# Attention over sorted edges: a fixed schedule of steps in place of a schedule of windows

## The reference

```python
q = (feats @ Wq.T + bq).reshape(bs, NHEAD, HDIM).transpose(1, 0, 2)
k = (feats @ Wk.T + bk).reshape(bs, NHEAD, HDIM).transpose(1, 0, 2)
v = (feats @ Wv.T + bv).reshape(bs, NHEAD, HDIM).transpose(1, 0, 2)
r, c = (edge_index[:, 0], edge_index[:, 1])
qe = q[:, c, :]
ke = k[:, r, :]
ve = v[:, r, :]
sim = jnp.einsum('hed,hed->eh', qe, ke) * scale
m = jax.ops.segment_max(sim, c, num_segments=bs)
p = jnp.exp(sim - m[c])
s = jax.ops.segment_sum(p, c, num_segments=bs)
attn = p / s[c]
out_e = attn.T[..., None] * ve
out_e = out_e.transpose(1, 0, 2).reshape(-1, NHEAD * HDIM)
agg = jax.ops.segment_sum(out_e, c, num_segments=bs)
return agg @ Wo.T + bo
```

## Time and profile before

| | |
|---|---|
| Median of 3 runs | 7157.06 us (7152.81 to 7159.54) |
| Profiled execution: its own time, its span | 7140.73 us, 7138.9 us |
| Mean granted clock of TensorE | 0.776 of full |
| Busy: PE, DVE, ACT, POOL | 4571.6, 4172.7, 2647.9, 4964.3 us |
| Attention stage | from about 3884 to 6942 us of the span |
| DMA | 1141.58 MB, mean 160 GB/s |

### The profile page before, as it was taken

The page is one execution under the profiler, slowest core; times in us unless marked ns, Lnnn a source line. Parts: engine busy times, 40 slices in busy tenths (PEclk is TensorE's granted clock), DMA queues, the critical chain, the costliest instruction groups (busy, mean ns, idle before and its releaser), DMA issues. The chain is left out here.

```text
span 7138.9 us, 97890 instructions
## 1 busy us (share of the span) xinstructions
PE 4571.6 (64%) x19401; PEld 3457.7 (48%) x19401; DVE 4172.7 (58%) x10973; ACT 2647.9 (37%) x9611; POOL 4964.3 (70%) x3907
## 2 busy tenths in 40 slices
PE   1466666666666656664994776677676767776767
PEld 1344444444444444443662555555554545554545
DVE  3643333333333333332666777878787878787866
ACT  0422222222222222221442555555555555555552
POOL 0688888888888888886553766766666667676740
PEclk6677777777777777776997778877878788788879
DMA  9777777777777777777864666666666666666646
GB/s 329 183 108 106 105 106 106 106 106 106 106 106 106 106 106 106 106 106 171 283 246 128 185 180 181 187 181 184 187 187 188 189 192 192 194 194 196 197 144 198
DMA packets 672062, 1141.58 MB, mean 160 GB/s; under 512 B 90146, under 2 KB 494828, under 8 KB 671478
## 3 DMA queue, kind: packets, MB, share of 16 engines
q0 software_dynamic: 381568, 691.69, 49.4%
q1 hardware_dynamic: 274835, 388.62, 17.7%
q10 hardware_dynamic: 15074, 54.95, 2.0%
HBM read 929.80 MB, written 464.23 MB: 195 GB/s over the span
## 5 line engine op out<-in xcount | busy, mean ns | idle before, releaser
L634 POOL DMA_INDIRECT sums<-mtw,posIw x1660 | 2593.6, 1562 | 607.7 <-issue 430.6
L1395 POOL DMA_INDIRECT kv<-kvt,sI x1760 | 1948.4, 1107 | 732.7 <-issue 413.6
L668 PE MATMUL ps<-h,wf 128*128 x3320 | 1340.1, 574 | 1149.3 <-ACT wf L693 1149.3
L1501 ACT ACTIVATE pv<-kv,pp 128x33 f32<-128x33 f32 x7040 | 1545.7, 308 | 755.0 <-PE ps L1436 751.3
L668 PEld LDWEIGHTS ps<-h,wf 128*128 128x128 f32 x3320 | 915.4, 289 | 1409.5 <-issue 1230.1
L702 ACT COPY mtw<-ps 128x512 f32<-128x512 f32 x830 | 485.7, 585 | 2339.0 <-DMA sums<-mtw,posIw 2254.8
L1419 PE MATMUL ps<-qb,OT 128*128 x5280 | 854.6, 325 | 423.5 <-DVE OT L1603 393.7
L1436 PE MATMUL ps<-pv,Of 128*128 128x264 f32 x3520 | 1089.6, 456 | 41.2 <-issue 32.0
L756 DVE TENSOR_TENSOR posIw<-step,sT 128x8 int32<-128x8 f32 x208 | 34.8, 167 | 1796.0 <-DMA sums<-mtw,posIw 1795.6
L1419 PEld LDWEIGHTS ps<-qb,OT 128*128 128x128 bf16 x5280 | 576.3, 112 | 638.8 <-issue 499.2
L1436 PEld LDWEIGHTS ps<-pv,Of 128*128 128x128 f32 x3520 | 749.5, 227 | 210.1 <-issue 70.6
(11 more groups left out here) (217 smaller groups left out, 4142.6 us busy)
## 6 DMA issues: line engine op xcount, KB each, us to landing
qb<-qt SPq DMA_DIRECT2D x880, 192.0 KB
accd<-acc SPq DMA_DIRECT2D x880, 132.0 KB
ints<-srows SPq DMA_DIRECT2D x208, 512.0 KB
dlr<-drows SPq DMA_DIRECT2D x110, 512.0 KB, 3.9
sums<-zero ACTq DMA_DIRECT2D x72, 704.0 KB, 19.6
part<-sums SPq DMA_DIRECT2D x56, 896.0 KB, 8.9
kv<-kvt,sI POOLq DMA_INDIRECT x1760
sums<-mtw,posIw POOLq DMA_INDIRECT x1660
```

The costliest lines, as they stand in the source:

```text
L634: e.indirect_dma_start(sums[j % NS], bass.IndirectOffsetOnAxis(ap=posI[:, j // W % 3, j % W:j % W + 1], axis=0), mt[:, j % NM, :], None, c ...
L668: m = e.matmul(psum[2 + q % 4][:, j % 2 * D:j % 2 * D + D], lhsT=BT[:, g % 3, j % 4, :], rhs=h[:, bass.ds(own[j % 4], 1), :].rearrange("p ...
L1395: e.indirect_dma_start(kv[:, s % NK, :], None, kvt, bass.IndirectOffsetOnAxis(ap=sI[:, s:s + 1], axis=0)).then_inc(kvs.sem(s), 16)
L1501: e.activation(pv[:, s % 8, h * 33:h * 33 + 33], kv[:, s % NK, D + h * 33:D + h * 33 + 33], ACT.Copy, scale=pp[:, w % 2, h, s % W2:s % W2 ...
```

## The change

All in the attention and its tables.

- The loops go over steps p, one group long, 440 + 9 of them, in place of windows. In step p DVE does `product(p)`, `reduce(p)`, `add(p - 9)`, and by p % 4 one part of the chain of window p // 4 - 1 (0: rescale of the window before it, columns of window p // 4 + 1, inner; 1: scale, across; 2: half of Of, outer; 3: other half of Of, scale). It scales group p - 7. PE does `expand(p + 1)`, one transfer of the chain (`turn`, `ends`, `spread`, `back`) and `agg(p - 8)`; `factor` of window p // 4 - 2 goes ahead in step 0. ACT scales group p - 7 around its parts of the chain; the exponential is first in step 3.
- Shares of scaling: of an even group DVE two slots and ACT two, of an odd group ACT three and POOL one (before: DVE 2 or 1, ACT 2, POOL 0 or 1).
- `kv` has 44 buffers (40), `qb` 8 (4), with the slot number of the accumulator in place of a row of its own. `OT` has 3 buffers (2), and the destinations are loaded straight into it and compared in place; `dlr` goes. Of is made in two halves from bf16 `iotab` and `dl2`; it stays f32. `abrow` is bf16.
- The factor moves from bank 4 to bank 5. SP: `rows` in step 1, `limits` in step 3, `flush` for groups p - 10 and p - 9.

```diff
-        NK, NQ, RB = 40, 4, 8
+        NK, NQ, RB = 44, 8, 8
         l1 = ExitStack()
-        dl2 = sb(l1, "dl2", [P, R2])
+        dl2 = sb(l1, "dl2", [P, R2], BF16)
...
-        abrow = sb(l1, "abrow", [1, NW2, 2, W2 + 1])
+        abrow = sb(l1, "abrow", [1, NW2, 2, W2 + 1], BF16)
...
-                e.tensor_scalar(irow[32:33, :], bi[32:33, :], NQ - 1, None, ALU.bitwise_and)
...
-            dlr = sb(stack, "dlr", [P, 2, W2 * P], BF16)
-            OT = sb(stack, "OT2", [P, 2, W2, P], BF16)
+            OT = sb(stack, "OT2", [P, 3, W2, P], BF16)
...
+
+            STEPS = NQD + 9
+
+            def shares(Q):
+
+                return ((0, 1), (2, 3), ()) if Q % 2 == 0 else ((), (0, 1, 2), (3,))
 
             def wait_weighed(e, Q):
-                e.wait_ge(S("l_wdve"), Q + 1)
-                e.wait_ge(S("l_wact"), act_weighed(Q))
+                e.wait_ge(S("l_wdve"), Q // 2 + 1)
+                e.wait_ge(S("l_wact"), NH * (5 * (Q // 2) + (2, 5)[Q % 2]))
...
-                        if w >= 2:
-                            e.wait_ge(S("l_ot"), w - 1)
-                        e.dma_start(dlr[:, w % 2, :], drows[0:1, w * W2 * P:(w + 1) * W2 * P].to_broadcast(
-                            [P, W2 * P])).then_inc(dls.sem(w), 16)
+                        if w >= 3:
+                            e.wait_ge(S("l_expanded"), 4 * (w - 3) + 4)
+                        e.dma_start(OT[:, w % 3, :, :].rearrange("p j e -> p (j e)"),
+                                    drows[0:1, w * W2 * P:(w + 1) * W2 * P].to_broadcast([P, W2 * P])).then_inc(
+                            dls.sem(w), 16)
...
-                for w in range(NW2 + 2):
-                    for u in range(4):
-                        if u == 0:
-                            rows(w + 2)
-                        if u == 1:
-                            limits(w)
-                        if u % 2 == 0 and 4 * w + u + 2 < NQD:
-                            queries((4 * w + u) // 2 + 1)
-                        Q = 4 * w + u - 7
-                        if Q >= 0 and Q % 2 == 1 and Q < NQD:
-                            flush(Q // 2)
+                for p in range(STEPS + 1):
+                    w, u = p // 4, p % 4
+                    if u % 2 == 0:
+                        queries(p // 2 + 1)
+                    if u == 1:
+                        rows(w + 2)
+                    if u == 3:
+                        limits(w)
+                    if u % 2 == 0 and 10 <= p < NQD + 10:
+                        flush((p - 10) // 2)
...
+                def weigh(Q):
+                    w = Q // 4
+                    for i in shares(Q)[2]:
+                        s = 4 * Q + i
+                        e.wait_ge(S("l_pp"), w + 1)
+                        if Q >= 2:
+                            e.wait_ge(S("l_summed"), 2 * Q - 2)
+                        e.tensor_tensor(pv[:, s % 8, :].rearrange("p (h d) -> p h d", h=NH),
+                                        kv[:, s % NK, D:KVW].rearrange("p (h d) -> p h d", h=NH),
+                                        pp[:, w % 2, :, s % W2:s % W2 + 1].to_broadcast([P, NH, 33]),
+                                        ALU.mult).then_inc(S("l_wpool"), 1)
...
+                for g in range(NQD + 10):
+                    if g >= 10:
+                        weigh(g - 10)
+                    if g < NQD:
+                        if g >= NK // 4:
+                            wait_weighed(e, g - NK // 4)
+                        for s in range(4 * g, 4 * g + 4):
+                            e.indirect_dma_start(kv[:, s % NK, :], None, kvt, bass.IndirectOffsetOnAxis(
+                                ap=sI[:, s:s + 1], axis=0)).then_inc(kvs.sem(s), 16)
...
+                def agg(Q):
...
+                    w = Q // 4
+                    e.wait_ge(S("l_of"), 2 * w + Q % 4 // 2 + 1)
+                    wait_weighed(e, Q)
+                    for j in (2 * Q, 2 * Q + 1):
+                        if j >= 2:
+                            e.wait_ge(S("l_add"), j - 1)
+                        for k in (2 * j, 2 * j + 1):
+                            m = e.matmul(psum[6 + j % 2][:, 0:NH * 33], lhsT=Of[:, w % 2, k % W2, :], rhs=pv[:, k % 8, :],
+                                         start=(k % 2 == 0), stop=(k % 2 == 1))
+                        m.then_inc(S("l_summed"), 1)
...
+                    if 0 <= v < NW2:
                         e.wait_ge(S("l_fa"), v + 1)
-                        e.wait_ge(S("l_of"), v + 1)
-                        e.matmul(psum[4][:, P + 8:P + 16], lhsT=ones[0:1, :], rhs=ones[0:1, 0:NH], start=True,
+                        e.wait_ge(S("l_of"), 2 * v + 1)
+                        e.wait_ge(S("l_pp"), v + 1)
+                        e.matmul(psum[5][:, 400:400 + NH], lhsT=ones[0:1, :], rhs=ones[0:1, 0:NH], start=True,
                                  stop=False)
-                        e.matmul(psum[4][:, P + 8:P + 16], lhsT=Of[0:1, v % 2, 0, :], rhs=x0[0:1, 2, :], start=False,
+                        e.matmul(psum[5][:, 400:400 + NH], lhsT=Of[0:1, v % 2, 0, :], rhs=x0[0:1, 2, :], start=False,
                                  stop=True).then_inc(S("l_factor"), 1)
...
+                expand(0)
+                for p in range(STEPS):
+                    w, u = p // 4, p % 4
+                    if u == 0:
+                        factor(w - 2)
+                    expand(p + 1)
+                    if u == 0:
+                        turn(w - 1)
+                    elif u == 1:
+                        ends(w - 1)
+                    elif u == 2:
+                        spread(w - 1)
+                    else:
+                        back(w - 1)
+                    agg(p - 8)
...
-                for w in range(NW2 + 2):
+                for p in range(STEPS):
+                    w, u = p // 4, p % 4
                     v = w - 1
                     on = 0 <= v < NW2
-                    weigh(4 * w - 6)
-                    if on:
+                    if u == 3 and on:
+                        e.wait_ge(S("l_td"), v + 1)
+                        if v >= 2:
+                            wait_weighed(e, 4 * v - 5)
+                        e.activation(pp[:, v % 2, :, :], psum[5][:, 2 * P:3 * P].rearrange("p (h j) -> p h j", h=NH),
+                                     ACT.Exp, scale=SCALE).then_inc(S("l_pp"), 1)
+                    weigh(p - 7, 0)
+                    if u == 1 and on:
...
+                    if u == 2 and on:
...
+                    weigh(p - 7, 1)
...
+                def rescale(v):
+                    if 0 <= v < NW2:
+                        places(8 * v)
+                        e.wait_ge(S("l_factor"), v + 1)
+                        if v:
+                            e.wait_ge(S("l_add"), 8 * v)
+                            e.wait_ge(flushed.sem(8 * v), flushed.value(8 * v - RB))
+                        to = acc[:, bass.ds(own[0], 1), :].rearrange("p a (h d) -> p (a h) d", h=NH)
+                        e.tensor_tensor(to, to, psum[5][:, 400:400 + NH].rearrange("p (h a) -> p h a", a=1).to_broadcast(
+                            [P, NH, 33]), ALU.mult).then_inc(S("l_rescale"), 1)
...
                     if w < NW2:
                         e.wait_ge(dls.sem(w), dls.value(w))
+                        at = OT[:, w % 3, :, :].rearrange("p j e -> p (j e)")
+                        e.tensor_scalar(at, at, icol[:, 0:1], None, ALU.is_equal).then_inc(S("l_ot"), 1)
+
+                def onehots(w, half):
+                    if 0 <= w < NW2:
                         if w >= 2:
-                            e.wait_ge(S("l_expanded"), 4 * w - 4)
-                        e.tensor_scalar(OT[:, w % 2, :, :].rearrange("p j e -> p (j e)"), dlr[:, w % 2, :],
-                                        icol[:, 0:1], None, ALU.is_equal).then_inc(S("l_ot"), 1)
-
...
+                            e.wait_ge(S("l_summed"), 8 * (w - 2) + 4 * half + 4)
+                            e.wait_ge(S("l_factor"), w - 1)
+                        j = half * (W2 // 2)
+                        n = W2 // 2
+                        e.tensor_tensor(Of[:, w % 2, j:j + n, :], bcast(iotab[:, :], n),
+                                        rows_of(dl2[:, w * W2 + j:w * W2 + j + n]), ALU.is_equal).then_inc(S("l_of"), 1)
...
+                def inner(v):
+
+                    if 0 <= v < NW2:
...
+                def across(v):
+
+                    if 0 <= v < NW2:
...
+                def outer(v):
+
+                    if 0 <= v < NW2:
...
+                for p in range(STEPS):
+                    w, u = p // 4, p % 4
+                    product(p)
+                    reduce(p)
+                    add(p - 9)
+                    if u == 0:
+                        rescale(w - 2)
+                        columns(w + 1)
+                        inner(w - 1)
+                    elif u == 1:
+                        weigh(p - 7)
+                        across(w - 1)
+                    elif u == 2:
```

(36 more changed lines are left out.)

124 lines of the change are left out of this document (21 added, 103 removed).

## The result

The changed kernel takes 6619.7 us (median of 4, 6613.9 to 6622.2) against 7158.2: ratio 0.9248, interval 0.9232 to 0.9264. The prediction was 6711, in a range of 6590 to 6925. The profiled execution took 6613.9 us, its span is 6612.1. Now and then an execution of any of these kernels falls into a slower state; all medians and ratios here leave those out.

A forecast was written before the change was run, and what follows sets the result against it. A loop of handovers bound the kernel before; POOL's gathers would after. 21.1 + 2.2 = 23.3 us per window against 27.48, over 109 periods, saves 456 us; with a +10 tail 6695, or 6711 by the median, range 6590 to 6925.

The forecast's parts named there:

- DVE bound, 21.5 to 22.6: Rival for the attention windows: holds fall between issues or Of gains from bf16; 21.5 to 22.6 us per window, chance 0.18.
- POOL is the bound after: Attention stage: POOL's 23.65 us per window, before adjusting its gathers for holds, exceeds DVE's 21.9, so its gathers decide.
- ACT's wait for the sums: Sign in the changed profile: ACT's wait for PE's sums falls from 6.8 to under 2 us per window.
- the hold: POOL's gathers lengthened by simultaneous DVE instructions: 2.2 us per window taken, between 1.8 and an unchanged 2.6.
- Holds as L x L / 2.5: Estimate of gather time lost to DVE instructions: 2.4 us per window before the change, 1.8 after, 0.60 per half of Of.
- DVE needs 21.9 us: DVE's work per attention window without waits, after the change: 21.9 - 0.85 + 0.7 + 0.15 = 21.9 us.
- bf16 columns bring nothing: Building Of from bf16 inputs: no gain taken, 1.22 us per half, since output stays f32 and one input is a broadcast.
- The step as walked: One 5.8 us step of the new order, walked across engines: the loops of waits open, each with 2 us or more in hand.
- the 11 us in hand: POOL's gathers with 44 buffers: a group's transfer has some 11 us to spare before it is wanted.
- PE's clock: Rival, with full locks: PE's clock at half level; half and half makes 24 to 25 us per window; joint chance 0.25.
- The slower rival: ACT keeps its waits for PE's sums and two more slots add 3.5: 31.0 us per window, about 7540 us, chance 0.09.
- The tail: End of the attention stage: two more steps without products, about +10 us.

## Why the prediction was right

- *No engine bound the kernel before; a loop did.* Borne out: one wait removed, a deeper ring and the new shares brought nothing or less than nothing in the old order, and the new steps with the old shares gave 0.9288.
- *Which case came.* The time lies in the range, but the 22.49 us per window lie below the forecast's 22.8 to 24.0 and in the case that I had called "DVE bound, 21.5 to 22.6", with its common rhythm.
- *POOL is the bound after.* Right for the first part of the stage. From about 4850 us on DVE is as full as POOL. The sum had put at nothing what POOL does to DVE: the columns took 1.026 us on average after 0.751, and 1.21 in the rhythm, so DVE needed 22.4 us there and not 21.9. The sign that DVE would have one large wait, for gathers, did not come: 27.6 us in the whole stage. ACT's wait for the sums, 2.3 us, stayed just over the 2 that I had named.
- *The term that was mis-sized is the hold.* I took 2.2 us per window, and it measured 1.46. 16 x 0.946 + 2 x 0.64 + 4.56 + 1.46 = 22.44, where the sum had 23.3; its 21.1 held POOL's scalings at 0.69 us each, so 0.12 of the holds stood in it twice. Between 23.3 and the 22.49 of the products are 0.81 us, x 109 = 88 us, and the prediction missed by 91. The rhythm is not the reason: between 4000 and 4800 us, ahead of it, the holds were 1.5 us too. There, by the DVE instruction that stood over the gather, they were 0.90 us per window under the halves of Of (1.20 in the sum), 0.30 under the columns (0.22) and 0.25 under DVE's scalings (0.40). In the rhythm about 0.5 are left on gathers and one scaling of POOL takes the other 1.0. The 1.8 of the rule was nearer than the 2.2 that I took; why it was still too much is open.
- *Holds as L x L / 2.5.* The rule gave 0.46 us per window for Of in one piece against two, measured (222.5 - 160.9) / 110 = 0.56. That difference came near; the whole did not, 1.8 against 1.46, and 2.4 against 2.58 for the gathers before.
- *DVE needs 21.9 us.* 21.95 by the kernel with the old shares.
- *bf16 columns bring nothing.* 1.218 us (median) for half of Of with bf16 inputs, 1.210 (mean) with the f32 row in PSUM.
- *The step as walked.* Right for PE and ACT; wrong for POOL, where the 11 us in hand did not exist. That this did not show is luck: the change happened to have 44 buffers, and with 40 the forecast would have been 94 us too low.
- *PE's clock* rose to 0.91, and this rival did not happen. The slower rival failed on its condition: ACT's wait for PE fell by 4.5 us per window.
- *The tail*: +6.7 us, +10 predicted.
- The Trainium skill (SBUF — State Buffer, Who interferes with whom) says that a DVE instruction with two SBUF inputs contends with a GpSimd instruction that reads SBUF. The PSUM operand shows it: with one SBUF input left, 77 us of holds (65 us of time) went. By its other rule, the loser blocked for the whole instruction, the sum would have been 25.7 us; the measured 22.44 speaks against it for gathers, most of which pass unheld: of 345 that overlap a half of Of, 266 take their usual 0.95 us. For the two meetings shown above it comes near: blocked to the other's end, POOL's scaling would take 1.15 + 0.64 = 1.79 us (1.63 measured) and the columns 0.64 + 0.75 = 1.39 (1.21 measured).

## What to carry to other kernels

When no engine is full, look for the loop and change the order: here a single wait taken out of it came back at other places, and work moved to an idle engine even cost time. Once the order is right, the fullest engines are the price of everything, and then their smallest terms count, here what the operand of one does to the other. When two engines come within a few tenths of a us of each other, ask what each does to the other's durations before calling one the bound. Ring depths must be counted from the time at which a full engine really starts, not from the earliest time at which it could.

## What the hardware showed that was not expected

- DVE and POOL fell into a fixed rhythm, window after window, in which POOL's 0.64 us scaling took 1.63 and DVE's 0.75 us columns 1.21. Both are full, and neither shows a wait for the other: the loss stands in the durations alone.
- A comparison with one operand moved from SBUF to PSUM kept its 1.21 us and took 77 us of holds off POOL (172.5 to 95.1).
- The scan of the runs takes 0.42 us in nearly every window now, after a median of 0.73, at equal size. The trace of before shows what stretched it: of its 220 scans (lines 1642 and 1644) the 210 that took over 0.55 us all overlap a scaling of POOL in time, and the 7 that overlap none took about 0.4. In the changed kernel none of the 220 overlaps one, and the longest takes 0.48.
